# Raw filter weights scaled behind attention units 2 and 3, and filter turns one unit later

## What is computed

```python
# layer 0, attention: 4 heads of 32; n = 256 tokens
q, k, v = split(_ln_c(x) @ w_qkv)
q = softmax(q, axis=-1) / sqrt(32)         # over the 32 channels of a head
k = softmax(k, axis=1)                     # over the tokens
context = einsum('bnhd,bnhe->bhde', k, v / n)
out = einsum('bhde,bnhd->bnhe', context, q) @ w_out + b_out
x = x + layernorm(out) * ln_scale

# layer 0, STU: four fractions (1, 1/2, 1/4, 1/8 of the tokens), 16 filters phi
for i, frac in enumerate((1, 2, 4, 8)):
    outs[i] = spectral(x[:, :T // frac], sigma, phi, M_phi_plus[i], M_phi_minus[i]) + ar(M_u[i], x)
y = softmax(log_weights + gumbel)
weights = one_hot(argmax(y)) - y + y
t = t + sum(outs * weights)
```

## Time and profile before

| what | value |
|---|---|
| median of 3 runs | 394.72 us (393.18 to 395.48) |
| time of the profiled execution | 395.31 us |
| its span in the trace | 393.4 us |
| mean granted TensorE clock | 0.971 of full speed |
| TensorE busy | 356.6 us, 91% of the span |
| VectorE busy | 229.0 us, 58% |
| ScalarE busy | 190.8 us, 48% |
| GpSimd busy | 33.0 us, 8% |

### The profile page before, as it was taken

One profiled execution on the slowest core, in us unless ns is written; L12 is line 12 of the kernel. 1 busy time (PEld: TensorE's weight loads), 2 busy tenths in 40 slices (PEclk: granted clock), 3 DMA queues, 4 the chain that ended last, 5 costly groups with the idle time before them and its releaser, 6 DMA issues.

```text
span 393.4 us, 9519 instructions
## 1 busy us (share of the span) xinstructions
PE 356.6 (91%) x4076; PEld 235.4 (60%) x4076; DVE 229.0 (58%) x456; ACT 190.8 (48%) x414; POOL 33.0 (8%) x39
## 2 busy tenths in 40 slices
PE   6966999999999899998988989899998899999891
PEld 2434565655555699974665359347745663774691
DVE  2577775858875622137845773662337267244885
ACT  2849678888658420016661736460247306024461
POOL 0026421212220000100000100000000000000000
PEclk9986999999999999999999999899999899999996
DMA  9982000000600000002000000000000000000004
GB/s 237 150 155 83 2 2 2 3 2 3 147 16 2 3 3 2 3 15 45 0 2 2 0 2 0 3 0 2 2 0 2 0 2 0 2 2 1 2 0 109
DMA packets 7338, 9.91 MB, mean 25 GB/s; under 512 B 3694, under 2 KB 6398, under 8 KB 6910
## 3 DMA queue, kind: packets, MB, share of 16 engines
q1 hardware_dynamic: 5630, 8.23, 10.3%
q10 hardware_dynamic: 1664, 1.05, 0.9%
HBM read 6.65 MB, written 1.05 MB: 20 GB/s over the span
## 4 chain that ended last, share of the span: by engine, by line
PE 62%; ACT 13%; DVE 12%; DMA 5%; issue 5%; SPq 2%; DVEq 0%; ACTq 0%
PE bank L651 28%; PE bank L1079 6%; DMA arena<-in_w_spec 5%; PE bank L274 5%; PE bank L268 4%; PE bank L1009 4%; PE bank L1020 4%; PE bank L851 2%; ACT lnv L373 2%; PE bank L875 2%; ACT arena L1244 1%; SPq L545 1%; ACT rs L378 1%; ACT arena L1246 1%; DVE arena L1752 1%
## 5 line engine op out<-in xcount | busy, mean ns | idle before, releaser
L367 ACT ACTIVATE sq<-bank 128x512 f32<-128x512 f32 x33 | 19.4, 591 | 66.7 <-PE bank L268 51.2
L651 PE MATMUL bank<-sb_consts 128*128 128x512 f32 (+1 forms) x96 | 43.7, 568 | 1.6 <-ACT arena L1445 1.6
L651 PE MATMUL bank<-xn,sb_w_attn 128*128 128x512 f32 x64 | 37.3, 667 | 6.2 <-ACT attn_scratch L1213 5.8
L274 PE MATMUL bank<-sq,sb_consts 128*128 128x512 f32 x66 | 34.7, 610 | 0.6 <-ACT sq L367 0.3
L373 ACT ACTIVATE lnv<-bank 128x512 f32<-128x512 f32 x33 | 19.7, 597 | 31.1 <-PE bank L274 30.9
L1079 PEld LDWEIGHTS bank<-arena,sb_w_late 128*128 128x128 f32 x180 | 23.0, 191 | 11.1 <-DVE arena L1811 8.0
L651 PE MATMUL bank<-arena 64*32 64x256 f32 (+4 forms) x466 | 26.6, 382 | 3.2 <-ACT arena L1246 2.2
L1079 PE MATMUL bank<-arena,sb_w_late 128*128 128x128 f32 x180 | 27.2, 287 | 1.7 <-DVE arena L1811 1.3
L1020 PE MATMUL bank<-arena,sb_w_late 128*128 128x128 f32 x144 | 27.9, 276 | 0.0
L1009 PE MATMUL bank<-arena,sb_consts 128*128 128x128 f32 x144 | 27.7, 276 | 0.1
L1382 ACT ACTIVATE arena<-bank 128x128 f32<-128x128 f32 x72 | 20.0, 278 | 13.9 <-PE bank L1020 13.7
(11 more groups left out here) (209 smaller groups left out, 624.5 us busy)
## 6 DMA issues: line engine op xcount, KB each, us to landing
arena<-in_w_spec SPq DMA_DIRECT2D x2, 720.0 KB
sb_w_late<-in_w_late SPq DMA_DIRECT2D x1, 1100.5 KB, 25.0
arena<-arena SPq DMA_DIRECT2D x4, 256.0 KB, 4.0
arena<-fourier SPq DMA_DIRECT2D x1, 768.0 KB, 22.7
sb_w_attn<-in_w_attn SPq DMA_DIRECT2D x1, 641.0 KB, 10.7
xR<-in_x SPq DMA_DIRECT2D x4, 128.0 KB, 3.9
xR<-in_x ACTq DMA_DIRECT2D x4, 128.0 KB, 4.1
arena<-in_w_spec SPq DMA_DIRECT2D x2, 256.0 KB
```

Source lines behind the costliest of these rows:

```text
L274: pe.matmul(bank[:, var_bank(i), :], mean32, sq[:, i % 2, :], start=True, stop=True)\
L367: act.activation(sq[:, i % 2, :], bank[:, centre_bank(i), :], ACT.Square).then_inc(S("ln_squared"), 1)
L651: return mm(ps, lhsT, rhs, start=True, stop=True)
```

## The change

ScalarE's two pairs of scales (fractions 0 and 1, fractions 2 and 3) stood at the head of its turns 2 and 3, before the query exponential; they now stand in the same turns behind the value copy. GpSimd's three sums stood behind the normalisations of units 0, 1 and 2; they now stand behind those of units 2, 3 and 4. FILT_FROM goes from 5 to 6, which moves the lags from unit 3 to 4, the spectra from unit 4 to 5 and the filter turns from units 5 to 12 to units 6 to 13. The dummy matmuls that stood in units 13 to 16 stand in 14 to 16. No load moves in its queue, and but for the one dummy matmul no instruction is added or taken away.

```diff
--- before.py
+++ after.py
@@ -44,7 +44,7 @@
 BUSY_ROW, BUSY_START, BUSY_BACK = 1, 3, 1
 BUSY_EXPERTS = (3, 1, 1, 3)
 WX_EARLY = [1, 2]
-FILT_FROM = 5
+FILT_FROM = 6
 BUSY_DRAIN = 1
 ACT_BD, ACT_BD_FIRST = 3, 2
 RES = 8
@@ -600,12 +600,10 @@
 
             for u in range(U):
                 q_normalise(u)
-                if u < FRACS - 1:
-
-                    pool.wait_ge(S("wm_scaled"), u + 2)
-                    m = wm_raw[:, u + 1, :]
-                    link(pool.tensor_tensor(m, m, wm_raw[:, u, :], ALU.add))
-                if u == FRACS - 2:
+                if 2 <= u < 2 + FRACS - 1:
+                    pool.wait_ge(S("wm_scaled"), u)
+                    link(pool.tensor_tensor(wm_raw[:, u - 1, :], wm_raw[:, u - 1, :], wm_raw[:, u - 2, :], ALU.add))
+                if u == FRACS:
                     pool.sem_inc(S("wm_seg"), 1)
 
 
@@ -794,7 +792,7 @@
                     attn_q_v(i)
                 if 0 <= i - 2 < U:
                     attn_ctx(i - 2)
-                if U - 4 < i <= U:
+                if U - 3 < i <= U:
                     pe.wait_ge(S("filt_sb"), C // 2)
                     keep_busy(BUSY_DRAIN, 4)
                 if i >= 3 and (i - 3) % NQ == NQ - 1:
@@ -1248,13 +1246,6 @@
                     .then_inc(S("filt_sb"), 1)
 
             for i in range(U + 3):
-                if i in (2, 3):
-
-                    act.wait_ge(S("w_spec_in"), 16 * len(FILTER_ROWS))
-                    act.wait_ge(S("fw_done"), 1)
-                    for n_ in (2 * i - 4, 2 * i - 3):
-                        act.activation(wm_raw[:, n_, :], wm_raw[:, n_, :], ACT.Copy, scale=fw[:, 7, n_:n_ + 1])\
-                            .then_inc(S("wm_scaled"), 1)
                 if 0 <= i - 1 < U:
                     a_q(i - 1)
                     a_kn(i - 1)
@@ -1275,6 +1266,12 @@
                     a_v(i)
                 if i == 0:
                     filter_setup()
+                if i in (2, 3):
+                    act.wait_ge(S("w_spec_in"), 16 * len(FILTER_ROWS))
+                    act.wait_ge(S("fw_done"), 1)
+                    for n_ in (2 * i - 4, 2 * i - 3):
+                        act.activation(wm_raw[:, n_, :], wm_raw[:, n_, :], ACT.Copy, scale=fw[:, 7, n_:n_ + 1])\
+                            .then_inc(S("wm_scaled"), 1)
                 for m in filter_turn(i, 1):
                     a_filters(m)
                 if i == U + 1:
```

## The result

The changed kernel takes 390.79 us (median of 8 runs, 389.33 to 398.69) against 394.87 us before: a ratio of 0.9904, with a 95% interval of 0.9877 to 0.9930. Two more sets of runs, made beside the experiments, gave 390.59 and 390.45 us, ratios 0.9895 (0.9869 to 0.9920) and 0.9900 (0.9865 to 0.9936). The forecast was 390.9. One of the 8 runs, the 398.69, was in a disturbed state; ratios leave such runs out.

A forecast was written before the change was run, and what follows sets the result against it. The raw filter weights' load, ahead in ScalarE's queue, was taken to bound the first units. 395.31 - 3.8 = 391.5 us for the profiled execution; with the median 0.6 lower, 390.9 us, range 389.6 to 393.0 (8 in 10).

The forecast's parts named there:

- k0: TensorE's first key projection, at 14.14 us in the kernel before; the forecast times are counted from it.
- k3: TensorE's key projection of unit 3: forecast to start at 31.0 us, 2.65 us earlier.
- k4: TensorE's key projection of unit 4: forecast to start at 35.8 us.
- k5: TensorE's key projection of unit 5: forecast at 40.75 us, the second scales costing 0.25 us there.
- k6: TensorE's key projection of unit 6: forecast at 46.95 us, behind the spectrum products of unit 5.
- first turn: First filter turn on TensorE, ahead of the value projection: due at 49.3 us, with a wait of 0.25 us.
- k14: TensorE's key projection of unit 14: forecast at 99.1 us instead of 102.91, 3.8 us less.
- The wait for the load: ScalarE's 4.25 us idle ahead of the scales, ended by the raw filter weights' landing at 29.37 us: forecast gone.
- The third sum: GpSimd's last fraction sum, forecast to end at 49.4 us, 49.5 with the signal, making TensorE wait 0.25 us.
- rival of a half clock: TensorE's clock at 0.50 for about 7 us in units 3 to 5: gain 2.3, 392.4 us; chance 10 in 100.
- another fall later: A later stage loses its clock too: 393.5 us; given back by this or a late load, 10 in 100.
- a plain unit of 4.59 us: Unit 13, without filter turns before: forecast to lose its 4.59 us, against 0.5 + 0.25 paid at the front.

The follow-up runs named there:

- e7: Changed kernel with VectorE's ten small fraction operations moved into turn 1, ahead of the query weights of unit 0; 390.70 us, 0.9889 of the kernel before.
- e4: Changed kernel with GpSimd's three sums one normalisation later, behind units 3 to 5; 397.61 us, 1.0069 of the kernel before.
- e5: The changed kernel run again, unaltered, on the chip of the next three runs; 390.59 us, 0.9895 of the kernel before.
- e3: Kernel before with three dummy matmuls of 512 columns on TensorE ahead of unit 3's key projection, the wait for the load left in; 393.82 us, ratio 0.9971.
- e1: Kernel before with only ScalarE's scales moved behind the value copies, sums and filter turns unmoved; 390.48 us, 0.9874 of the kernel before.
- e6: Kernel before with only the scales moved, run again beside the changed kernel on one chip; 390.84 us, 0.9909 of the kernel before.
- e9: Kernel before with SyncE's two loads behind the raw weights issued only when the raw weights have landed; 394.27 us, 0.9980 of the kernel before.
- e2: Kernel before with only the filter turns moved to units 6 to 13, scales and sums unmoved; 394.41 us, 0.9988 of the kernel before.
- e11: The changed kernel run a third time, unaltered; 390.45 us, 0.9900 of the kernel before.
- e10: Changed kernel with the fraction operations early and the two loads behind the raw weights held back until these land; 390.85 us, 0.9909 of the kernel before.
- e12: Kernel before with only the scales moved, plus fraction operations early and the two loads behind the raw weights held back; 390.49 us, 0.9885 of the kernel before.

## Why the prediction was right, point by point

The instruction that held the first units was named rightly, and the steps can be held against the rows when both are counted from k0 (the prediction's times less 14.14, the change's less 13.45):

| step | forecast | measured |
|---|---|---|
| k3 | 16.9 | 16.87 |
| k4 | 21.7 | 21.78 |
| k5 | 26.6 | 26.72 |
| k6 | 32.8 | 32.90 |
| first turn | 35.4 | 35.72 |
| k14 | 85.0 | 85.23 |

**The wait for the load** is gone and the fraction weights are late next, as forecast: e7 moved them and k3 came 1.1 us earlier. **The first scales** are hidden and the second hold the query exponential. **The third sum**: a wait of 0.25 us was forecast and 0.40 measured, and e4 showed that such a wait is paid in full. **The eight units with turns** were forecast to keep their 51.89 us; from k6 (46.35) with the wait of 0.40 to k14 (98.68) they took 51.93 beside it. **The filter copies** stayed covered: their first reader, at 136.63 us, shows no idle ahead of it, and SyncE's eight issues stood at 100.44. **The clock** stayed at 1.00 from k3 to k14, so the rival of a half clock did not come about there. The longer fall in the experts, 1.28 us in this profile, is what that rival called another fall later, but e5, with the change too, did not have it. e3 priced what the clock had cost before.

Three things were weaker than the text made them look. First, the prediction's account of the gain, a plain unit of 4.59 us that goes from the end against 0.75 us paid at the front, is right as a sum but not as a cause. The move of the turns takes a plain unit of 4.59 us from the end and puts one at the front: k4 to k5 in the change, 4.94 us, with the second scales in it (the unit with the spectra takes 6.18 us, from 36.74 to 42.92 in e1 and from 40.17 to 46.35 in the change). Here that is 0.35 us lost, with the 0.40 us of the sum 0.75, and e1 and e6, which leave the turns where they were, are 0.3 and 0.8 us nearer from k0 to k14. What gains is that the scales, with their wait and the clock behind it, left the front. Moving the turns buys nothing that these runs can tell.

Second, the first units were called bound by the load. In the profile of before the load ended ScalarE's wait, but only 0.17 us behind the fraction weights, which the scales need too; with the load in early (e9) k3 stayed 19.4 us behind k0, and with the scales moved it came to 16.87. So of these 2.6 us nearly all came from the scales' place in the queue: their wait for the fraction weights and their own 2.19 us stood ahead of the query exponential, the key copy and the key exponential, and the first two of these now run while VectorE makes the fraction weights (26.46 to 27.58). In other executions the load held longer: in e2 it ended the wait at 31.59, where the fraction weights were done at 27.75. The move takes all of this off the path, so the sum came out either way.

Third, the start of k0 was taken as fixed. It wandered from 11.88 to 14.49 us in these executions and the load's landing from 29.1 to 31.6. Before the change the later of the landing and the fraction weights set the time; after it, k0 does. That the medians came out at 4.1 to 4.3 us less and the rows at 3.5 is within this, and that the median lies within 0.1 us of the forecast is in part luck. (The chances for a gain within 0.5% and for a slower kernel, 0.14 and 0.05, add up to 0.15 and 0.04 from the parts given.)

## What to carry to other kernels

Where a load holds an engine that works in strict order, look at who stands behind it in the queue, and move the waiting instruction behind the work that needs no load. Count its other waits and its own length too: here an earlier load alone gained nothing clear, and the move gained 1%. The clock that TensorE loses in such a gap comes on top, here some three tenths to a half of the gain. Before the removal, look for the next wait that ends within a microsecond of it: there the gain stops. And when a change has two parts, run each alone: here one of them carried all of it.

## What the runs showed of the hardware

- **The same gap cost the clock in one execution and not in another.** In all 14 profiles TensorE idles 2.60 or 2.61 us ahead of k2. In 8 of them k2 or the query projection behind it was slowed (the query projection took 2.03 us before, 2.07 in e6, 1.83 in e11); in the other 6 it took 1.12 or 1.13 us, as in the change's first profile, the same kernel as e11. By the Trainium skill, page "TensorE: Matmul & The Clock Gate" (Part 1: The HAM clock gate), the window in which activity is watched runs freely; these runs agree with it.
- **Later loads delay an earlier one on the same queue.** The raw weights landed at 25.9 to 27.0 us when the two loads behind them were held back (e9, e10, e12), and at 29.1 to 31.6 us in the five other profiles in which the scales waited for them. In e9 the mean busy share of the 16 DMA engines fell to 0.30 from 22 to 23 us and to between 0.08 and 0.14 from 23 to 26, and SyncE issued no other load until 27.03, so the last part of this load kept only a few engines busy. The Trainium skill's page "DMA: Bandwidth & Descriptors" (Queues, rings and completion order) says that each DMA engine takes its descriptors in the ring's order and that a copy may use fewer than all engines. The share in e9 agrees with the second; the first would not by itself give the delay. Which engines these loads used was not measured, so the cause stays open.
- **A wait for GpSimd can be called "issue".** TensorE's 0.40 us in the change and 5.25 us in e4 stood under this name, though the sum that they waited for is in GpSimd's rows.
